# Copying every second group's transposed exponentials out of PSUM on VectorE instead of ScalarE, in a fused two-layer kernel

## What is computed

```python
def step(h, inp):                 # layer 0: scan over 512 tokens
    dA_t, dBu_t = inp
    h = dA_t * h + dBu_t
    return (h, h)
...
scores = jnp.einsum('bhqd,bhkd->bhqk', q, k) / math.sqrt(HEAD_DIM)   # layer 1: 16 heads of 8
scores = scores + _sliding_window_mask(s, WINDOW_SIZE)               # |i - j| <= 32
probs = jax.nn.softmax(scores, axis=-1)
attn = jnp.einsum('bhqk,bhkd->bhqd', probs, v)
```

## Time and profile before

| | before |
|---|---|
| median of three runs | 1017.35 us (1017.04 to 1018.69) |
| the profiled execution | 1021.74 us |
| its span in the trace | 1019.9 us |
| busy PE / PEld / DVE / ACT / POOL | 810.4 / 560.0 / 760.9 / 638.1 / 434.0 us |
| mean granted PE clock | 0.91 of full speed |
| attention of sequences 0 to 6 | from 283 us to 931 us of the span, seven turns of 92 to 105 us |

### The profile page before, as it was taken

One profiled execution on the slowest core, in us unless ns is written; L12 is line 12 of the kernel. 1 busy time (PEld: TensorE's weight loads), 2 busy tenths in 40 slices (PEclk: granted clock), 3 DMA queues, 4 the chain that ended last, 5 costly groups with the idle time before them and its releaser, 6 DMA issues.

```text
span 1019.9 us, 15614 instructions
## 1 busy us (share of the span) xinstructions
PE 810.4 (79%) x5226; PEld 560.0 (55%) x5226; DVE 760.9 (75%) x1059; ACT 638.1 (63%) x1976; POOL 434.0 (43%) x248
## 2 busy tenths in 40 slices
PE   1855788776788788988898799889888986899785
PEld 0622787664554565556555656565556554556443
DVE  7769443445867897789778977897888888786475
ACT  0233566644579566956795689568956884595554
POOL 2368331104564156516742573266426632571100
PEclk9957899998789888999999989999999998899898
DMA  6564799775434254235414541464145414550000
GB/s 218 172 193 137 233 280 299 225 203 132 119 79 98 60 143 99 64 103 145 115 46 120 149 99 41 119 152 106 32 123 148 106 41 124 129 122 15 19 11 12
DMA packets 85952, 123.20 MB, mean 121 GB/s; under 512 B 8560, under 2 KB 43760, under 8 KB 85744
## 3 DMA queue, kind: packets, MB, share of 16 engines
q1 hardware_dynamic: 79584, 115.38, 41.6%
q0 software_dynamic: 6288, 6.82, 3.0%
HBM read 106.21 MB, written 12.29 MB: 116 GB/s over the span
## 4 chain that ended last, share of the span: by engine, by line
PE 36%; DVE 24%; ACT 14%; issue 12%; POOL 8%; DMA 3%; SPq 1%; DVEq 0%; POOLq 0%; ACTq 0%
DVE hst L818 9%; PE more L1446 6%; ACT pexp L1118 5%; PE y_bank L1314 5%; DVE dBu L810 5%; POOL xs_d L1184 3%; ACT dA L1040 3%; POOL hc L1216 3%; ACT pT L1131 2%; PE work L1333 1%; PE work_l L1458 1%; PE work L1359 1%; PE work L1496 1%; PE work_l L1428 1%; PE work L1292 1%
## 5 line engine op out<-in xcount | busy, mean ns | idle before, releaser
L1216 POOL TENSOR_TENSOR hc<-hst,bcr 128x1024 f32<-128x1024 f32 x116 | 273.7, 2360 | 423.1 <-DVE dBu L810 401.6
L818 DVE TENSOR_TENSOR_SCAN hst<-dA,dBu 128x1024 f32<-128x1024 f32 x128 | 291.8, 2280 | 1.9 <-ACT dA L1040 0.9
L1040 ACT ACTIVATE dA<-dt,neg_a 128x511 f32<-128x511 f32 x256 | 171.0, 726 | 34.0 <-DVE hst L818 31.4
L810 DVE TENSOR_TENSOR dBu<-dtu,bcr 128x1024 f32<-128x1024 f32 x128 | 160.4, 1253 | 11.9 <-DMA bcr<-bc_d 1.5
L1314 PE MATMUL y_bank<-pk,hc 128*128 128x128 f32 x1024 | 153.9, 299 | 14.5 <-POOL hc L1216 10.9
L1314 PEld LDWEIGHTS y_bank<-pk,hc 128*128 128x128 f32 x1024 | 128.8, 154 | 50.8 <-issue 23.3
L1446 PE MATMUL more<-pk,pexp 128*96 128x128 f32 x480 | 109.4, 301 | 48.5 <-ACT pexp L1118 43.0
L1446 PEld LDWEIGHTS more<-pk,pexp 128*96 128x96 f32 x480 | 58.1, 129 | 95.4 <-issue 51.9
L1118 ACT ACTIVATE pexp<-work,nmax 128x96 f32<-128x96 f32 x240 | 77.9, 337 | 30.8 <-DVE nmax L965 30.7
L1131 ACT COPY pT<-more 96x512 f32<-96x512 f32 x120 | 69.9, 582 | 36.8 <-PE more L1446 36.3
L965 DVE TENSOR_REDUCE nmax<-work 128x4 f32<-128x384 f32 x60 | 33.4, 557 | 78.3 <-PE work L1367 57.5
(11 more groups left out here) (363 smaller groups left out, 1524.7 us busy)
## 6 DMA issues: line engine op xcount, KB each, us to landing
bcr<-bc_d SPq DMA_DIRECT2D x128, 512.0 KB, 5.1
qbd<-in_wx SPq DMA_DIRECT2D x8, 578.0 KB, 4.6
o_all<-in_wx SPq DMA_DIRECT2D x8, 578.0 KB, 4.8
pT<-in_wx SPq DMA_DIRECT2D x8, 578.0 KB, 5.1
kT<-in_wx SPq DMA_DIRECT2D x8, 578.0 KB, 5.1
vw<-in_wx SPq DMA_DIRECT2D x8, 578.0 KB, 5.0
xs_d<-rbuf POOLq DMA_DIRECT2D x1, 2560.0 KB, 9.7
hst<-in_hidden SPq DMA_DIRECT2D x8, 256.0 KB, 6.6
```

The source lines that it names most:

```text
L810: v.tensor_tensor(dBu[:], dtu[par], bcr[n % RING][:, 0:1, :].to_broadcast([P, NH, L]), ALU.mult).then_inc(s_dBu, 1)
L818: v.tensor_tensor_scan(hst[n % 2][:].rearrange("p h t -> p (h t)"), dA[n % 2][:].rearrange("p h t -> p (h t)"), dBu[:].rearrange("p h t -> ...
L1040: s.activation(dA[n % 2][:, h, 1:L], dt[par][:, h, 1:L], ACT.Exp, scale=neg_a[:, h, n:n + 1]).then_inc(s_dA, 1)
L1216: g_.tensor_tensor(hc[n % 2][:], hst[n % 2][:], bcr[n % RING][:, 1:2, :].to_broadcast([P, NH, L]), ALU.mult).then_inc(s_hc, 1)
```

## The change

A new helper says which copies move: those of odd groups, for all sequences but the last. In VectorE's program the unit "turn" now waits for PE's transposes, copies them into pT and frees the bank; ScalarE leaves out these copies. The place in program order stays the plan's: the unit "turn" comes after "rowmax" and before the rest of the slot.

```diff
+        def dve_turns(b, k):
+            return b < B - 1 and k % 2 == 1
...
                     v.tensor_reduce(nmax[:, k, :], w1k(b, f"s{k}")[:, 0:RG * KW].rearrange("p (r k) -> p r k", r=RG),
                                     AX_X, ALU.max, negate=True).then_inc(s_nmax, 1)
+                elif name == "turn" and dve_turns(b, k):
+                    full1(dve, b, f"pT{k}")
+                    v.tensor_copy(pT[k % 4][:], w1k(b, f"pT{k}")[0:KW, :]).then_inc(free1(b, f"pT{k}"), 1)
                 elif name == "rden":
...
-                elif name == "turn":
+                elif name == "turn" and not dve_turns(b, k):
                     full1(act, b, f"pT{k}")
                     s.copy(pT[k % 4][:], w1k(b, f"pT{k}")[0:KW, :]).then_inc(free1(b, f"pT{k}"), 1)
```

## The result

The changed kernel takes 1077.28 us (median of four runs, 1076.84 to 1077.48) against 1018.02 us (median of four) for the kernel before: ratio 1.0573, 95% interval 1.0552 to 1.0594. It is 59 us slower where 45 were forecast; 1077.28 lies just above the range's upper end of 1076. Its profiled execution took 1077.23 us with a span of 1075.4, 55.5 above the span before. VectorE is busy 34 us longer (795.3 for 760.9), ScalarE 25 us less (613.2 for 638.1), PE 24 us longer (834.5 for 810.4); the waits show where the rest comes from.

A forecast was written before the change was run, and what follows sets the result against it. No engine is full; a chain of waits binds. Turns 1 to 6 add 38.4 us and turn 7 adds 7: +45.4 on the profiled 1021.74, 1067.1, less 4.4 to the median: 1062 us, range 1044 to 1076.

The forecast's parts named there:

- the ring: Loop between odd groups' exponentials through VectorE's waiting copy: 1.81 + 0.60 + 3.53 + 0.59 = 6.53 us, minimum per pair of slots.
- which pairs are spared: Turn 6, pairs 7 to 9 and 9 to 11: 6.55 and 7.51 us before, forecast neither loss nor gain.
- the five lengthened pairs of turn 6: Pairs 1 to 3, 3 to 5, 5 to 7, 11 to 13, 13 to 15: +1.39, +1.25, +1.30, +1.36, +1.07 us.
- the turn's tail: After group 15: copy and y_out delay the last scan; 0.76 us gets through, short waits take some: +0.6 us.
- the last of the part on the change: PE's longer waits might lower its clock; pair 13 to 15 keeps 1.00, so nothing was added to the sum.
- The lower clock: Rival: PE falls to 1.2 GHz in lengthened turns, 24 us more, 1086, or 1074 for half the pairs; chance 0.13.
- the prediction's signs of being wrong: Scans starting before the copy's wait ends, turn 7 pairs near 5.4 us, or granted clocks below 1.00 in middle pairs.
- the estimate of 6.4 a turn: Mean loss in us over turns 1 to 6, 38.4 us in all; below turn 6's 7.0, as some pairs were already longer.
- Turn 7 with its end: Five pairs growing from 5.41 to 6.53 us make 5.6, plus 1.4 for the last two and the tail: 7 us.
- I carry this over: The runs' median lay 4.4 us below the profiled execution; the same gap was taken off 1067.1, giving 1062.
- the absorbing turn boundary: Rival: next turn's early slots wait for something unmoved, returning 1.5 to 3 us a turn: 1040 to 1048; chance 0.13.
- ScalarE's relief: Rival: taking copies off ScalarE shortens the chain, at most 32.6 us, about 20: 997 us; chance 0.04.

The follow-up runs named there:

- The runs with the clock held up: Changed kernel with idle PE time filled by unread identity transposes: 1064.28 us; kernel before, filled likewise at the start of a turn: 1013.51 us.
- the filled kernels: Kernel before and changed kernel, each with unread identity transposes put into idle PE time: 1013.51 us and 1064.28 us.
- behind the scan: Changed kernel with odd groups 1 to 13 copied by VectorE after the next slot's scan, group 15 by ScalarE again: 1031.86 us, ratio 1.0156.
- another kernel: Kernel before plus, in each odd slot, a VectorE maximum of the copy's length that waits for nothing: 1043.83 us, ratio 1.0240.

## Why the prediction was right and wrong

Right: that it gets slower, by the wait and not mainly by the copy; that the ring runs scan, dBu, maxima, exponentials, transposes, copy; its price of 6.53 (pairs 3 to 11 of turn 7: 6.51 to 6.65); which pairs are spared; and three of the five lengthened pairs of turn 6, and the turn's tail (+0.6), to 0.1 us or better.

Wrong: the size, 1077.28 for 1062, and the step that failed is the last of the part on the change. "In pair 13 to 15 PE is busy only 6.18 of 7.63 us and keeps 1.00, so I count none of it in the sum." In the sum's own terms, the 3.62 us after which PE delivers group 1's transposes (at 792.62) became 4.56, and the 3.12 from the even to the odd exponentials in pair 5 to 7 became 4.19, both at the lower clock. Pair 13 to 15 was the wrong witness: it keeps 1.00 after the change too, at 6.18 of 8.70. Two better ones were in the trace of before. In pair 1 to 3 the clock was already falling after the 1.84 us wait, and in turn 1 its second wait has the full 1.42 us: that pair took 9.15 there, against 7.55 in turn 6. And the 8.37 us of turn 4's pair 13 to 15, read as a pair that happens to be longer, stand behind a pair of 7.63 us at a granted clock of 0.78: a middle pair had lost the clock without any change.

The lower clock was named, and put down as a rival at 13 in 100 with 1074 to 1086. That the time lies in there is in part luck: the rival's price was made of the dt projection in pairs 7 to 9 and 9 to 11, which stayed at 1.00 (6.54 and 7.51), and of 0.3 us in every other pair; what came is about 1 us in each of two pairs, and nothing in turn 6's pair 11 to 13. One of the prediction's signs of being wrong did show, granted clocks below 1.00 in the middle pairs.

The ledger, profile against profile: +55.5 us measured, +45.4 forecast, so 10.1 short. Turns 1 to 6 lengthened by 45.5 for 38.4. By the prediction's own terms, pair by pair, it would be about 36.6 (so the estimate of 6.4 a turn was 1.8 high); over the six turns pair 1 to 3 lost 5.1 us more than these terms give and pair 5 to 7 lost 4.1 more, the rest next to nothing together. Turn 7 with its end took 9.3 for 7. Its first five pairs took 5.4 for 5.6, though not as was thought: only four of them stood at 5.41, the first at 6.74. The last two and the end took 3.9 for 1.4, the largest part of the excess in pair 11 to 13 (7.76 for 6.10, after a PE wait of 1.52, then scores at 1.48). The last 0.7 came ahead of turn 1.

The runs with the clock held up show, and don't only argue, that the clock lengthens the two pairs: 8.59 and 7.48 us. But not all the 13.0 us that they give back are a price of the change, for the kernel before gets 5.6 back too (1019.1 to 1013.5). Between the filled kernels the change still costs 50.8 us, so by this measure the clock's share of the 59 is some 8. Turns 1 to 6 lengthen there by 41.2, 6.9 each: no first pair is long before, so every turn loses what turn 6 was forecast to lose (7.0).

The other 5 us of the 15 are the step "I carry this over" (4.4) and a rounding down. The profiled execution of before had its own slow place, turn 4 (8.36, 7.63 and 8.37 in three pairs, against 7.55, 6.82 and 7.63 in turn 6), which may be 2.4 of the 4.4 us by which it lay above the median; this isn't shown, as no other execution of that kernel has a trace. The changed kernel's execution lies on its median (1077.23, 1077.28), so nothing was to be subtracted.

Of the other rivals, the absorbing turn boundary fell: exponentials of group 15 to those of the next group 0 took 48.94 for 48.34 in turn 6, and 0.66 more on the mean of six turns (from 0.84 less to 1.40 more). ScalarE's relief fell as argued. Where relief could work, behind the scan, it brought turn 7's pairs from 5.41 to 5.3, and the other turns paid for it at the shared bank and by the lower clock.

The Trainium skill (TensorE: Matmul & The Clock Gate, What's actually happening) has the throttled clock as the default that activity releases; the filled kernels agree, with 1.00 for 0.65 in pair 1 to 3. The prediction had this rule beside its sum and gave it no term.

## What to carry to other kernels

Idle time ahead of a wait is not room for another instruction: look whether that instruction's input is there when the engine comes to it, and what stands behind it in program order. A sum of waits should be costed at both clocks of PE: where a change lengthens PE's waits, look in the trace for the stretch that already has such waits, not for one that is merely less busy. And in a kernel whose PE waits at the start of each round, a few matmuls into a free bank can pay by themselves, here 0.6%.

## What the runs showed that was not expected

- Fourteen transposes a turn that compute nothing made the kernel before 0.64% faster (0.9917 to 0.9956), mostly by pair 1 to 3: 7.21 us in place of 7.55 to 9.21 makes 6.2 of the 6.8 us between the two spans.
- A VectorE product with both inputs in SBUF took 0.68 us by itself, 1.93 beside a product of POOL that had started before it, up to 2.60, and 1464 ns on the mean of 56; POOL's product took 2359 ns, as in the filled kernel of before (2360). A VectorE maximum with one such input took 672 ns throughout. The Trainium skill (Advanced Engine Details and Errata, GPSIMD Details) says that POOL and VectorE conflict where a VectorE instruction has two SBUF inputs; the trace agrees, and here VectorE alone paid for it (in the rows shown POOL's product had started first).
- PE waits of like length (1.37 and 1.38 us ahead of group 11) left the clock at 1.00 in five turns of the kernel before, and let it fall in the sixth and in another kernel; what decides is open.
